# Values products of two attentions as four 32-column array tiles, normalised once per group of graphs

## The reference, cut to what matters

```
# first attention (graph attention), on layernorm(x)
h = (x @ W.T) as 4 heads of 32
e = leaky_relu(a_src + a_dst.T, 0.2), masked by adj
x = x + softmax(e) @ h            # 128x128 probabilities, 32 features, per head
# second attention, causal, with rotary terms, on rmsnorm(layernorm(x))
scores = q @ k.T / sqrt(32); y = softmax(scores) @ v
x2 = z + y @ wo.T
# experts: top 2 of 8, hidden size 341
out = x2 + sum_e weight_e * (silu(f @ w1_e.T) * (f @ w3_e.T)) @ w2_e.T
```

## Time and profile before

| what | value |
|---|---|
| median of three runs | 1989.12 us |
| profiled execution, its own time | 1984.17 us |
| its span, first to last instruction | 1982.4 us |
| PE busy | 1698.9 us, 86% |
| weight loads busy | 1308.2 us, 66% |
| DVE busy | 1450.5 us, 73% |
| ACT busy | 926.4 us, 47% |
| POOL busy | 958.7 us, 48% |
| mean granted TensorE clock | 0.956 of full speed |

### The profile page before, as it was taken

How to read it: one execution, slowest core, us unless ns; L and a number is a source line. 1 busy time by engine, 2 the same in 40 slices (tenths; PEclk the granted TensorE clock), 3 DMA queues, 4 the chain that set the end, 5 groups by cost and what they waited for, 6 DMA issues and landing times.

```text
span 1982.4 us, 39651 instructions
## 1 busy us (share of the span) xinstructions
PE 1698.9 (86%) x10546; PEld 1308.2 (66%) x10546; DVE 1450.5 (73%) x5051; ACT 926.4 (47%) x2779; POOL 958.7 (48%) x852
## 2 busy tenths in 40 slices
PE   3667777999999999999999999999999999988675
PEld 2545566777777777777777777777777777766343
DVE  3556666878888788788887888888888888865532
ACT  1344433555555554555554555445555555543121
POOL 1143466554445555555544555545555444554433
PEclk9888888999999999999999999999999999988897
DMA  4000111222222212222222222122222222212221
GB/s 121 7 26 20 37 33 37 43 40 41 43 41 43 43 34 37 45 43 42 42 42 41 41 44 43 31 41 44 44 40 43 42 44 40 38 34 40 38 32 18
DMA packets 142416, 79.26 MB, mean 40 GB/s; under 512 B 33048, under 2 KB 137564, under 8 KB 141949
## 3 DMA queue, kind: packets, MB, share of 16 engines
q0 software_dynamic: 47232, 34.92, 12.2%
q1 hardware_dynamic: 94973, 41.80, 8.4%
HBM read 33.39 MB, written 44.86 MB: 39 GB/s over the span
## 4 chain that ended last, share of the span: by engine, by line
PE 54%; DVE 20%; issue 8%; POOL 4%; ACT 4%; DMA 1%; DVEq 0%; POOLq 0%; SPq 0%; ACTq 0%
PE bank L1056 7%; PE bank L1075 6%; PE bank L967 5%; PE bank L1060 5%; PE bank L893 5%; PE bank L1068 4%; PE bank L980 4%; PE bank L1002 3%; PE bank L1009 2%; DVE z L638 2%; PE bank L929 2%; DVE hg L858 2%; POOL routed L398 2%; DVE fx L660 2%; PE bank L1019 1%
## 5 line engine op out<-in xcount | busy, mean ns | idle before, releaser
L419 POOL DMA_INDIRECT out<-ys,xt x264 | 426.3, 1615 | 519.3 <-DMA out<-ys,xt 252.6
L398 POOL DMA_INDIRECT routed<-fx,slot x256 | 256.2, 1001 | 141.5 <-DVE slot L779 77.5
L503 ACT ACTIVATE p<-ub,nm 128x128 f32<-128x128 f32 x512 | 163.6, 390 | 277.4 <-DVE nm L712 277.4
L1075 PE MATMUL bank<-w_s,hsT 128*128 (+1 forms) x1584 | 232.1, 283 | 27.8 <-ACT hsT L545 20.4
L858 DVE SCALAR_TENSOR_TENSOR hg<-sg,bank 128x341 f32<-128x341 f32 x264 | 134.7, 510 | 163.2 <-ACT sg L538 161.8
L1075 PEld LDWEIGHTS bank<-w_s,hsT 128*128 128x128 f32 (+1 forms) x1584 | 205.2, 193 | 68.5 <-issue 61.4
L1056 PE MATMUL bank<-w_s,xT 128*128 x528 | 218.4, 496 | 19.6 <-DVE xT L852 7.7
L1060 PE MATMUL bank<-w_s,xT 128*128 x528 | 202.7, 466 | 4.0 <-DVE hu L866 0.4
L511 ACT ACTIVATE p<-bank,nm 128x128 f32<-128x128 f32 x512 | 145.5, 365 | 118.1 <-DVE nm L718 118.0
L544 ACT ACTIVATE hsT<-bank 128x256 f32<-128x256 f32 x264 | 101.1, 383 | 154.0 <-PE bank L1068 152.8
L1068 PE MATMUL bank<-ident,hu 128*128 128x128 f32 (+1 forms) x792 | 136.3, 282 | 33.1 <-DVE hu L866 15.7
(11 more groups left out here) (172 smaller groups left out, 3484.4 us busy)
## 6 DMA issues: line engine op xcount, KB each, us to landing
xt<-routed SPq DMA_DIRECT2D x264, 65.0 KB, 1.8
xs<-in_x SPq DMA_DIRECT2D x32, 256.0 KB, 3.1
out<-bs SPq DMA_DIRECT2D x32, 256.0 KB, 2.3
out<-ys,xt POOLq DMA_INDIRECT x264, 3.4
routed<-fx,slot POOLq DMA_INDIRECT x256
w_s<-in_w SPq DMA_DIRECT2D x2, 1364.0 KB
adj<-in_adj SPq DMA_DIRECT2D x32, 64.0 KB, 3.3
w_s<-in_w SPq DMA_DIRECT2D x2, 512.0 KB
```

The source lines that it names most:

```text
L398: pool.indirect_dma_start(routed, bass.IndirectOffsetOnAxis(slot[p][:, i:i + 1], 0), fx[i // GB][p][:, i % GB, :], None).then_inc(S[f"sc{p ...
L419: pool.indirect_dma_start(out_rows, bass.IndirectOffsetOnAxis(xt[r][:, C:C + 1].bitcast(I32), 0), ys[r][:], None, compute_op=ALU.add).then ...
L503: last = act.activation(p1[j % 2][:, h, :], ub[j % 2][:, h, :], ACT.Exp, bias=nm1[:, j, h:h + 1])
L1075: last = pe.matmul(y_p[:, 0:C], hsT[r % 2][0:n, c, :], w2_s[0:n, bass.ds(e, 1), c, :].rearrange("p a c -> p (a c)"), start=c == 0, stop=c ...
```

## The change

- `values1` and `values2` exchange the operands: the values of a head (128x32) are stationary and the transposed probabilities (128x128) stream. Each head writes its own 32 partitions of the bank, so the four products of a graph use four column tiles of the array, each 32 columns wide. The result is transposed: features on partitions, tokens along the row. Only 128 columns of the bank are written.
- ACT copies each result out, per graph, to ogT or yU.
- The row sums come from the exponentials: `accum_out` on each of the 32 exponential instructions of a period, to sum1 and sum2. The columns of ones and their memsets are gone, and hE and vE are contiguous.
- First attention: when the four graphs of a group are there, the new step G.ot transposes ogT back on PE (four transposes), DVE takes the 16 reciprocals and multiplies the group in one instruction (og), and POOL adds the group in one instruction.
- Second attention: the new step A.rb on DVE takes the 16 reciprocals and spreads them over the heads' features into riE. T.yT transposes riE on PE in the place of y, and DVE multiplies the transposed reciprocals with yU and has yT. ACT's copy L435 is gone.
- `mix` (two DVE instructions per graph and attention) is gone. The release of bank g2 for the next graph's transposes comes from ACT's copy and no longer from DVE.
- ORDER is written anew.

```
-ORDER = """T.yT G.xn A.hN E.l.0 E.l.1 E.x.0 G.h E.u.0 E.g.0 E.l.2 G.p1.0 E.t.0 E.x.1 A.q E.u.1 T.wo E.g.1 G.p1.1 E.x.2 T.ms E.s.0 A.kr E.d.0 A.k E.u.2 G.o1.0
...
+ORDER = """G.xn G.h A.hN E.x.0 T.yT E.l.0 E.u.0 E.l.1 E.g.0 T.wo E.x.1 G.p1.0 A.q T.ms E.u.1 E.t.0 G.p1.1 E.s.0 E.l.2 E.d.0 E.x.2 E.g.1 A.k A.kr E.u.2 G.o1.0
...
-M.na E.s.5 A.o2.3 E.t.7 A.v2.3 E.d.7 E.s.6 E.l.7 E.s.7""".split()
...
+A.v2.2 E.g.7 E.t.7 E.s.5 M.na E.s.6 A.o2.3 E.d.7 E.s.7 A.v2.3""".split()
...
-                def v1(j):
-                    pool.wait_ge(S["og"], 4 * g + j + 1)
-                    if j == 0 and late(g, 2):
+                def ot():
+                    pool.wait_ge(S["og"], g + 1)
+                    if late(g, 2):
                         pool.wait_ge(S["hN"], 4 * (g - 1))
                         pool.wait_ge(S["base"], g - 1)
-                    pool.tensor_tensor(x1[p][:, j, :], xs[p][:, j, :], og[:, j, :], ALU.add).then_inc(S["x1"], 1)
+                    pool.tensor_tensor(x1[p][:], xs[p][:], og[:], ALU.add).then_inc(S["x1"], 1)
...
-                        act.activation(hE[:, 2 * i:2 * i + 2, 0:NH * GW].rearrange("p b (h w) -> p b h w", w=GW)[:, :, :, 0:HD + 1],
-                                       gp[i][:, 0:2 * NH * (HD + 1)].rearrange("p (b h w) -> p b h w", b=2, h=NH),
-                                       ACT.Copy).then_inc(S["hE"], 1)
+                        act.activation(hE[:, 2 * i:2 * i + 2].rearrange("p b h w -> p (b h w)"),
+                                       gp[i][:, 0:2 * NH * GW], ACT.Copy).then_inc(S["hE"], 1)
...
+                    if late(g, 1) and j == 0:
+                        act.wait_ge(S["ri1"], g)
                     for h in range(NH):
-                        last = act.activation(p1[j % 2][:, h, :], ub[j % 2][:, h, :], ACT.Exp, bias=nm1[:, j, h:h + 1])
+                        last = act.activation(p1[j % 2][:, h, :], ub[j % 2][:, h, :], ACT.Exp, bias=nm1[:, j, h:h + 1],
+                                              accum_out=sum1[:, j, h:h + 1])
...
+                def values1(j):
+                    act.wait_ge(S["pv1"], 4 * g + j + 1)
+                    if late(g, 1):
+                        act.wait_ge(S["og_ps"], g)
+                    act.activation(ogT[:, j, :], g2[:, 0:L], ACT.Copy).then_inc(S["ogT"], 1)
+
+                def values2(j):
+                    act.wait_ge(S["pv2"], 4 * a + j + 1)
+                    if late(a, 2):
+                        act.wait_ge(S["yT"], a - 1)
+                    act.activation(yU[pa][:, j, :], a1[:, 0:L], ACT.Copy).then_inc(S["y"], 1)
...
-                def mix(j, ps, pv, ri, s_ri, dst, s_dst, one, n):
-
-                    dve.wait_ge(S[pv], 4 * n + j + 1)
-                    dve.reciprocal(ri[:, j, :], heads(ps, one, 1).rearrange("p h a -> p (h a)")).then_inc(S[s_ri], 1)
-                    dve.wait_ge(S[s_ri], 4 * n + j + 1)
-                    dve.tensor_tensor(dst[:, j, :].rearrange("p (h d) -> p h d", h=NH), heads(ps, 0, HD),
-                                      ri[:, j, :].unsqueeze(2).broadcast_to([L, NH, HD]), ALU.mult).then_inc(S[s_dst], 1)
-
-                def mix1(j):
-                    if late(g, 1) and j == 0:
-                        dve.wait_ge(S["x1"], 4 * g)
-                    mix(j, g2, "pv1", ri1, "ri1", og, "og", GW - 1, g)
-
-                def mix2(j):
-                    if late(a, 2) and j == 0:
+                def ot():
+                    dve.wait_ge(S["e1"], 4 * g + 4)
+                    if late(g, 1):
+                        dve.wait_ge(S["x1"], g)
+                    dve.reciprocal(ri1[:], sum1[:]).then_inc(S["ri1"], 1)
+                    dve.wait_ge(S["ri1"], g + 1)
+                    dve.wait_ge(S["og_ps"], g + 1)
+                    dve.tensor_tensor(og[:].rearrange("p b (h d) -> p (b h) d", h=NH),
+                                      g2[:].rearrange("p (n d) -> p n d", d=HD),
+                                      ri1[:].rearrange("p b h -> p (b h)").unsqueeze(2).broadcast_to([L, GB * NH, HD]),
+                                      ALU.mult).then_inc(S["og"], 1)
+
+                def rb():
+                    dve.wait_ge(S["e2"], 4 * a + 4)
+                    if late(a, 2):
                         dve.wait_ge(S["yT_ps"], a - 1)
-                    mix(j, a1, "pv2", ri2, "ri2", y[pa], "y", HD, a)
+                    dve.reciprocal(ri2[:], sum2[:]).then_inc(S["ri2"], 1)
+                    dve.wait_ge(S["ri2"], a + 1)
+                    dve.tensor_copy(riE[pa][:].rearrange("p b (h d) -> p (b h) d", h=NH),
+                                    ri2[:].rearrange("p b h -> p (b h)").unsqueeze(2).broadcast_to([L, GB * NH, HD])).then_inc(S["riE"], 1)
+
+                def yT_():
+                    dve.wait_ge(S["yT_ps"], t + 1)
+                    dve.wait_ge(S["y"], 4 * t + 4)
+                    if late(t, 1):
+                        dve.wait_ge(S["wo_ps"], t)
+                    dve.tensor_tensor(yT[:].rearrange("c b l -> c (b l)"), t2[:], yU[p][:].rearrange("c b l -> c (b l)"),
+                                      ALU.mult).then_inc(S["yT"], 1)
...
-                    pe.wait_ge(S["y"], 4 * t + 4)
+                    pe.wait_ge(S["riE"], t + 1)
                     if late(t, 1):
                         pe.wait_ge(S["route"], ROUTE * t)
-                    flip(t2, y[p]).then_inc(S["yT_ps"], 1)
+                    flip(t2, riE[p]).then_inc(S["yT_ps"], 1)
+
+                def ot():
+                    pe.wait_ge(S["ogT"], 4 * g + 4)
+                    flip(g2, ogT).then_inc(S["og_ps"], 1)
...
-                        pe.wait_ge(S["og"], 4 * g + j)
+                        pe.wait_ge(S["ogT"], 4 * g + j)
...
                     pe.wait_ge(S["pT1"], 4 * g + j + 1)
                     for h in range(NH):
-                        o = h * (GW - SKEW)
-                        last = pe.matmul(g2[:, h * 128:(h + 1) * 128], pT1[j % 2][:, h, :], hE[:, j, o:o + 128], start=True, stop=True)
+                        last = pe.matmul(g2[h * HD:(h + 1) * HD, 0:L], hE[:, j, h, 0:HD], pT1[j % 2][:, h, :], start=True, stop=True)
                     last.then_inc(S["pv1"], 1)
 
                 def values2(j):
                     pe.wait_ge(S["pT2"], 4 * a + j + 1)
                     for h in range(NH):
-                        o = h * (HW - SKEW)
-                        last = pe.matmul(a1[:, h * 128:(h + 1) * 128], pT2[j % 2][:, h, :], vE[:, j, o:o + 128], start=True, stop=True)
+                        last = pe.matmul(a1[h * HD:(h + 1) * HD, 0:L], vE[:, j, h * HD:(h + 1) * HD], pT2[j % 2][:, h, :], start=True, stop=True)
```

More of the change, by code:

```diff
@@ L32 @@
 NG = B // GB
-GW, HW = HD + 2, HD + 1
-SKEW = HD - 1
+GW = HD + 1
 HC = [(0, 128), (128, 128), (256, HID - 256)]
@@ L149, in gnn_moe_block @@
         p1, pT1 = two("p1", [L, NH, L]), two("pT1", [L, NH, L])
-        ri1, og = sb("ri1", [L, GB, NH]), sb("og", [L, GB, C])
+        sum1, ri1 = sb("sum1", [L, GB, NH]), sb("ri1", [L, GB, NH])
+        ogT, og = sb("ogT", [C, GB, L]), sb("og", [L, GB, C])
         x1 = two("x1", [L, GB, C])
@@ L158, in gnn_moe_block @@
         kbd = sb("kbd", [C, GB, NH, L])
-        vE = sb("vE", [L, GB, NH * HW + 2])
+        vE = sb("vE", [L, GB, C])
         nm2 = sb("nm2", [L, GB, NH])
         p2, pT2 = two("p2", [L, NH, L]), two("pT2", [L, NH, L])
-        ri2, y = sb("ri2", [L, GB, NH]), two("y", [L, GB, C])
+        sum2, ri2 = sb("sum2", [L, GB, NH]), sb("ri2_", [L, GB, NH])
+        riE, yU = two("riE", [L, GB, C]), two("yU", [C, GB, L])
         yT, x2, sq = sb("yT", [C, GB, L]), sb("x2", [L, GB, C]), sb("sq", [L, GB, C])
@@ L201, in gnn_moe_block @@
         names = """ld_c ld_w prep0 prep prep_ps half_ ready wscale xl0 xl1 al0 al1
-        mask st_g mv_g ve_g rstd xn xnT_ps xnT hp_ps hE P_ps t u m1 e1 pT1_ps pT1 pv1 ri1 og x1
+        mask st_g mv_g ve_g rstd xn xnT_ps xnT hp_ps hE P_ps t u m1 e1 pT1_ps pT1 pv1 ogT og_ps ri1 riE og x1
         st_a mv_a va norm_a z hN hT_ps hT proj qa qb qT ka kb kk kd kp vE s_ps m2 e2
@@ L420, in scatter @@
                                             ys[r][:], None, compute_op=ALU.add).then_inc(S["zs"], 16)
-                return {"nx": nx, "na": na, "ms": ms_, "v1": v1, "sc": sc, "s": scatter}
+                return {"nx": nx, "na": na, "ms": ms_, "ot": ot, "sc": sc, "s": scatter}
             phase1(pool, steps)
@@ L428, in steps @@
             def steps(g, p):
-                a, t = g - 1, g - 2
-                def yT_():
-                    act.wait_ge(S["yT_ps"], t + 1)
-                    if late(t, 1):
-                        act.wait_ge(S["wo_ps"], t)
-                    act.activation(yT[:].rearrange("c b l -> c (b l)"), t2[:], ACT.Copy).then_inc(S["yT"], 1)
+                a, t, pa = g - 1, g - 2, 1 - p
                 def xn_():
@@ L462, in v @@
                         act.wait_ge(S["pv2"], 4 * a)
-                    act.activation(vE[:, :, 0:NH * HW].rearrange("p b (h w) -> p b h w", w=HW)[:, :, :, 0:HD],
```

(12 more changed lines are left out.)

30 lines of the change are left out of this document (12 added, 18 removed).

## The result

The changed kernel took 2077.1 us, median of 4 runs (2063.3 to 2079.24), beside 1988.8 us for the kernel before: ratio 1.0437, interval 1.0392 to 1.0482. That is slower, and outside the range.

| session | changed kernel | interval of the ratio | kernel before |
|---|---|---|---|
| first | 2077.1 us | 1.0392 to 1.0482 | 1988.8 us |
| third | 1921.0 us | 0.9613 to 0.9673 | 1990.5 us |
| fourth | 1919.9 us | 0.9615 to 0.9728 | 1991.8 us |
| fifth | 2076.4 us | 1.0383 to 1.0451 | 1992.1 us |

A forecast was written before the change was run, and what follows sets the result against it. PE was taken to bound the steady part. Per period PE -1.0, DVE -0.4, ACT +0.4, turn +0.3 and crumbs -0.4 made -1.1 us, times 32 -35: 1949 profiled, 1954 us median, range 1865 to 2045.

The forecast's parts named there:

- The sum: Whole run: the per-period terms add to -1.1 us, times 32 is -35, giving 1954 us; chance 0.40.
- a period over 55 us: Sign for the steady part: the forecast is wrong if a period is under 52 or over 55 us.
- Rival 2: Values products on PE: it empties at both tile changes, nothing overlaps; 2063 us, 2000 to 2090, chance 0.20.
- The values group: Eight records on PE: five distances (0.555) plus one emptying (0.167), 0.72 us instead of 0.89, saving 1.4 a period.
- rival 1: Values products on PE: all tiles run at once, PE 46.6 us busy a period; 1893 us, 1840 to 1925, chance 0.25.
- all my other terms: Per period, beside PE's -1.0 us: DVE -0.4, ACT +0.4, turn +0.3, order's idle crumbs -0.4.
- Rival 3: PE's saving comes back as waits and a lower clock, so no change; 1990 us, 1975 to 2005, chance 0.15.
- DVE, 43.8 forecast: DVE's busy time a period: mix goes (3.7 us), 2.1 to 2.4 added, from 45.1 to 43.8 us.
- ACT, 33 forecast: ACT's busy time a period: 2.1 us of copies and 3 of accumulator reads added, 28.4 to about 33 us.
- the charged 0.4: Later exponentials on ACT delay the tanh and copies queued behind: +0.4 us a period, range 0 to 3.
- The turn: Longer chain to hN offset by a moved projection: +0.3 us a period, -1.5 to +1.5; PE waits about 2.9.
- The order: The rewritten order may remove PE's idle crumbs: -0.4 us a period, range 0 to 1.0.

The follow-up runs named there:

- e8: The changed kernel with whole-array values products, each head's block padded by zeros and the heads added in the bank, reference's result kept: 2077.5 us, ratio 1.0439.
- e9: The changed kernel again, nothing altered, in the third session: 1921.0 us, ratio 0.9643 to the kernel before.
- e11: The changed kernel with whole-array values products, heads overwriting each other so values are not the reference's, third session: 1948.1 us, ratio 0.9799.
- e10: The changed kernel without accum_out in both attentions, sums constant 1 and outputs not normalised, third session: 1909.7 us, ratio 0.9601.
- e14: The changed kernel in the old order, with G.ot and A.rb put in behind E.t.6, fourth session: 2146.4 us, ratio 1.0789.
- e7: The changed kernel with accum_out in the first attention only, the second's sums constant 1 and its result not normalised: 2072.0 us, ratio 1.0415.
- e5: The changed kernel without the turn_dve semaphore increments on DVE, for which nobody waits: 2068.3 us, ratio 1.039.
- e6: The changed kernel with the loads and norm of the next group moved later, behind E.g.5: 2101.4 us, ratio 1.0553.
- e18: The changed kernel with the spreading copy to riE on GpSimd instead of VectorE, fifth session: 2067.2 us, ratio 1.0399.

## Why the prediction was wrong

**The recorded run: a step that wasn't there.** Every rival let an engine wait for another's work. None had the hand-over itself take longer. The sum took it as in the trace before, where no update of PE comes late, and put nothing for it. It measured 3.4 and 3.8 us at two hand-overs of a period. Per period the disturbed level costs 57.59 less 52.36, 5.2 us, and 32 of these are 167; the times differ by 156. By the prediction's own sign, a period over 55 us, the forecast is wrong there (57.00); the quiet 52.36 is just inside. Rival 2 ended at 2063 us, near the result, but that is luck, since its mechanism is refuted: a group costs 0.45 at most, and e8 without tiles is as slow.

**The values group: 0.72 taken, 0.45 measured for one that stands alone.** My step said that the two records of a head can't be at once, which made five distances (0.555), and added one emptying (0.167). The emptying is near the 0.22 of both changes. The streaming is what was wrong: in e9 four records start within 0.02 us of each other and the other four 0.11 us behind them, and the whole takes 0.24. Four tiles stream side by side, as rival 1 had it, though it had nothing for the changes. The estimate of 0.37 from the Trainium skill, "TensorE: Matmul & The Clock Gate", Part 3 (three tiles, 512 streamed columns), lies between the 0.35 of a group in a pair and the 0.45 of a single one. A period has eight groups in seven stretches, 8 x 0.24 + 7 x 0.22 = 3.5 us where 7.1 stood: 3.6 us saved by this estimate, where I had 1.4. Rival 1's 46.6 us of PE meets the measured 46.5 in part by luck: it took 4.9 off 51.5, and the stretches above give 4.1 off 50.7.

**What of it comes through.** Rival 1 let 3 us through. A quiet period is 2.3 us shorter altogether, and tiles against whole array (e11, e9) 27 us / 32 = 0.85. In my own terms: PE's busy time fell by 4.1 where I had 1.0, and its idle time rose by 1.9 where all my other terms came to -0.1. PE now idles 5.8 us a period. Rival 3's idea, the gain coming back as waits, holds for nearly half of it; its clock doesn't (0.99 in the quiet stretch, as before).

**DVE, 43.8 forecast, 43.8 measured,** but the agreement is luck. I took 1.4 off 45.1; measured are 0.8 off 44.6. The spreading copy by itself is at the lower end of what I had (0.43); left out was POOL's addition beside it, which makes it 1.46. The two reciprocals took 0.24 each, not 0.175. On POOL rr rose from 1.69 to 1.93, and what lengthens it was not looked for.

**ACT, 33 forecast, 31.7 measured.** The records of the reads sum to about 145 us in 23 periods, 6.3 each, but most of it lies over the next exponential. Two exponentials start 0.34 and 0.39 us apart (second and first attention), without reads 0.25 and 0.29 (e10), so a read adds 0.09, 2.9 us a period; I had taken 3. Of that 11 us / 32 = 0.35 a period is paid, near the charged 0.4. That price was measured in the new order alone. In the old one DVE waits 3.0 us a period longer for ACT's tanh than before (e14); how much of this is the reads' was not run.

**The turn, +0.3 forecast in one wait of 2 to 4 us.** There is no such wait; xn takes 1.12 us a period, and the rest is spread over kbd, xnT, hu and hsT.

**The order, -0.4 for crumbs.** The wrong kind of term. Its worth depends on the operations: +50 us on the old ones, -226 on the new (2146.4 to 1919.9).

In a quiet session the sum, 1954, is 33 us too high, and its own range (1925 to 1980) misses 1920 by 5. Two slips carry nothing: with 0.44 us for G.ot over eight groups, rival 2's turning point is 0.84, not 0.87, and 0.40, 0.25 and a third of 0.15 make 0.70, not 0.69.

**Open.** What disturbs a session, and which half of the change makes the kernel sensitive to it. No kernel in the old order was in a disturbed session except the one before. Excluded as necessary: the tiles (e8), the second attention's reads (e7), the turn's updates (e5), the place of the loads and norm (e6), the spreading copy on VectorE (e18). PE is dense there (3.82 us busy of the 4 from 999 to 1003), but it is so in quiet sessions and before as well. Every run on record carries a span and a clock of the profiler, and updates are missing from the trace in the same stretches, so it isn't excluded that the recording takes part. No version that beats the kernel before in both kinds of session was found; in quiet ones the changed kernel is the fastest of those that compute the whole reference.

## What to carry to other kernels

Price column tiles by the distance between starts: four 32-column products side by side cost about as much as one (0.24 against 0.22 us), and the changes to and from the whole array 0.1 us each, which is as much again for a group that stands alone. So put such groups side by side in the order. Operations and their order are one edit: either half alone was slower here by 2.6 to 8%, both together faster by 3.5%. And when an engine starts microseconds after the end of what it waits for, with the releaser unknown to the trace, repeat both kernels in another session before explaining the difference by the code.

## What was not expected of the hardware

The hand-over of a result from PE, counted from the modelled end of the matmul, took 0.04 us in one session and 3.4 us at the same place in another, for the same program, the longest 10.5 us. By the times, it came in every run of a session or in none. A VectorE copy of 128x512 with a broadcast source took 0.43 us by itself and 1.46 with an addition of 128x512 on GpSimd beside it, while the addition kept its length (1.28 us, and 1.27 for an operation of that size before). Reading the accumulator takes 187 to 202 ns, but lies beside the next exponential, which it puts off by 0.09 us.
